# Moments and normalization of the first batch's x in the setup block, V's low weights on GpSimd, Wk loaded first

## What is computed

```
emb = silu(sin_emb(timestep)) @ W_ada + b_ada; scale, shift = split(emb)
x = ln(src) * (1 + scale) + shift
q, k, v = x @ Wq + bq, x @ Wk + bk, x @ Wv + bv
probs = softmax(where(mask, -inf, q k^T / sqrt(32) + attention_bias))
x = x + (probs v) @ Wo + bo
out = rotate(x + gelu2(ln(x) * g2 + beta2 @ W1 + b1) @ W2 + b2)
```

## Time and profile before

| | us |
|---|---|
| median of 3 runs | 3292.41 (3285.91 to 3293.02) |
| the profiled execution's own time | 3286.79 |
| its span | 3285.0 |
| PE busy | 3159.6 (96%) |
| POOL, DVE, ACT busy | 2015.2, 2141.5, 1859.9 |
| DMA queue of SP | 79.3% of the span |

### The profile page before, as it was taken

The page is one execution under the profiler, slowest core; times in us unless marked ns, Lnnn a source line. Parts: engine busy times, 40 slices in busy tenths (PEclk is TensorE's granted clock), DMA queues, the critical chain, the costliest instruction groups (busy, mean ns, idle before and its releaser), DMA issues. The chain is left out here.

```text
span 3285.0 us, 52375 instructions
## 1 busy us (share of the span) xinstructions
PE 3159.6 (96%) x16592; PEld 2373.3 (72%) x16592; DVE 2141.5 (65%) x4445; ACT 1859.9 (57%) x4041; POOL 2015.2 (61%) x1247
## 2 busy tenths in 40 slices
PE   5999999999999999999969999999999999999998
PEld 4777777777777777767638688787877868687787
DVE  3777778777777777877757654554645555464542
ACT  2777777777777777777725243342434434253443
POOL 3888888888878888878745633435333443434413
PEclk9999999999999999999989999999999999999999
DMA  5999999998999999998857677675767757586665
GB/s 188 263 267 272 261 274 279 263 265 270 261 271 267 268 261 264 275 270 261 259 157 269 211 246 222 188 254 180 256 205 221 243 185 247 181 261 207 200 204 166
DMA packets 440432, 785.15 MB, mean 239 GB/s; under 512 B 57024, under 2 KB 106176, under 8 KB 440160
## 3 DMA queue, kind: packets, MB, share of 16 engines
q1 hardware_dynamic: 440160, 781.82, 79.3%
HBM read 591.76 MB, written 89.19 MB: 207 GB/s over the span
## 5 line engine op out<-in xcount | busy, mean ns | idle before, releaser
L671 POOL TENSOR_TENSOR biasm<-biasm,maskb 128x1024 f32<-128x1024 f32 x512 | 1091.8, 2152 | 241.6 <-DMA biasm<-in_fside_Bx16xSxS_dram 238.4
L1388 PE MATMUL ps_out<-w_ring,g_hi 128*128 128x512 f32 x2048 | 678.7, 398 | 15.9 <-POOL w_ring L1625 7.9
L1368 PE MATMUL ps_first<-h_hi,w_ring 128*128 128x512 f32 x1792 | 553.4, 390 | 7.5 <-issue 7.4
L1607 POOL TENSOR_TENSOR g_lo<-g_now,g_hi 128x512 fp32r<-128x512 f32 x128 | 169.3, 1323 | 618.1 <-ACT g_hi L1485 618.1
L776 PE MATMUL ps_score<-k_rows,q_rows 96*128 96x512 f32 x1024 | 493.1, 482 | 3.7 <-issue 3.3
L1388 PEld LDWEIGHTS ps_out<-w_ring,g_hi 128*128 128x128 f32 x2048 | 385.6, 188 | 110.4 <-issue 30.8
L827 ACT ACTIVATE probT<-ps_probT 128x512 f32<-128x512 f32 x512 | 305.2, 596 | 239.6 <-PE ps_probT L789 162.2
L917 DVE CUSTOM_DVE_ANT_0 prob_first<-ps_score,biasm 128x512 f32<-128x512 f32 x512 | 346.9, 684 | 142.7 <-PE ps_score L776 104.0
L917 DVE CUSTOM_DVE_ANT_0 prob_last<-ps_score,biasm 128x512 f32<-128x512 f32 x512 | 346.5, 686 | 139.1 <-PE ps_score L776 109.6
L789 PE MATMUL ps_probT<-ident,prob_first 128*128 128x128 f32 x2048 | 392.9, 273 | 16.8 <-DVE probT L496 10.4
L1388 PE MATMUL ps_out<-w_ring,g_lo 128*128 128x512 f32 x1024 | 399.7, 390 | 0.0
(11 more groups left out here) (159 smaller groups left out, 5606.8 us busy)
## 6 DMA issues: line engine op xcount, KB each, us to landing
biasm<-in_fside_Bx16xSxS_dram SPq DMA_DIRECT2D x512, 512.0 KB, 7.2
w_ring<-w_parts SPq DMA_DIRECT2D x240, 512.0 KB, 3.7
w_ring<-w_parts SPq DMA_DIRECT2D x392, 256.0 KB, 3.5
k_rows<-k_hi SPq DMA_DIRECT2D x512, 64.0 KB, 6.0
q_rows<-q_hi SPq DMA_DIRECT2D x512, 64.0 KB, 4.0
xn<-in_x_dram SPq DMA_DIRECT2D x16, 1024.0 KB, 8.0
normal_rows<-xn SPq DMA_DIRECT2D x16, 1024.0 KB, 9.2
k_rows<-k_lo SPq DMA_DIRECT2D x256, 64.0 KB, 5.6
```

The costliest lines, as they stand in the source:

```text
L671: pool.tensor_tensor(tile, tile, maskb[:, 2 * half:2 * half + 2, :], ALU.add).then_inc(masked.sem, 1)
L1368: mm = pe.matmul(ps[:, BANK[n], :], w1r[:, place, w, cols], h[:, n, c, :], start=(c == 0 and k == 0 and not onto), stop=(c == 1 and k == 2 ...
L1388: mm = pe.matmul(ps_out[:, t, :], a[:, k % 2, cols], w2r[:, k % VR, w, :], start=(m == 0 and n == 0), stop=(m == NF - 1 and n == 2))
L1607: pool.tensor_tensor(GLO[:, k % 2, :], src, GHI[:, k % 2, :].bitcast(F32), ALU.subtract).then_inc(glo_done.sem, 1)
```

## The change

In the setup block, after the modulation's activations, DVE takes batch 0's moments, adds EPS, and, between K's low weights and Q's, normalizes `xn` in place; the power is POOL's. POOL also makes V's low weights. SP loads Wk ahead of Wq, and ACT and DVE treat K first (ACT scales Wq when its turn comes). START no longer does the moments, the power and the normalization of batch 0; the later batches are as before. DVE increments a semaphore where it has waited for the power (`dve_waited`, bookkeeping alone).

```diff
@@ setup_block, SP
                 load_x(sp, 0)
-                for n in range(3):
+                for n in (1, 0, 2):
                     sp.dma_start(wst[:, n, :, :], ...).then_inc(w_in[n], 16)
@@ setup_block, POOL
+                eps_added.wait(pool, -1, 0)
+                pool.tensor_tensor(rstd[:, :], var_eps[:, :], half_pow[:, :], ALU.pow).then_inc(pow_done.sem, 1)
+                pool.wait_ge(scaled, 1 + NC * 3)
+                for c in range(NC):
+                    pool.tensor_tensor(WL[2][:, c, :], wst[:, 2, c, :], WH[2][:, c, :].bitcast(F32), ALU.subtract)
@@ setup_block, DVE
-                for n in range(3):
-                    dve.wait_ge(scaled, 1 + NC * (n + 1))
+                x_in.wait(dve, -1, 0)
+                for t in range(NC):
+                    dve.bn_stats(stats[:, t, :], xn[:, t, :]).then_inc(stats_made.sem, 1)
+                stats_made.wait(dve, -1, NC - 1)
+                for t in range(NC):
+                    dve.bn_aggr(mean_var[:, t, :], stats[:, t, :]).then_inc(stats_done.sem, 1)
+                stats_done.wait(dve, -1, NC - 1)
+                dve.tensor_scalar(var_eps[:, :], mean_var[:, :, 1], EPS, None, ALU.add).then_inc(eps_added.sem, 1)
+                for n in (1, 0):
+                    dve.wait_ge(scaled, (1 + 2 * NC, NC)[n])
                     for c in range(NC):
                         dve.tensor_tensor(WL[n][:, c, :], wst[:, n, c, :], WH[n][:, c, :].bitcast(F32), ALU.subtract)
+                    if n == 1:
+                        pow_done.wait(dve, -1, 0)
+                        dve.sem_inc(dve_waited, 1)
+                        for t in range(NC):
+                            dve.tensor_scalar(xn[:, t, :], xn[:, t, :], mean_var[:, t, 0:1], rstd[:, t:t + 1],
+                                              ALU.subtract, ALU.mult).then_inc(normed.sem, 1)
@@ setup_block, ACT
-                act.wait_ge(w_in[0], 16)
-                act.mul(wst[:, 0, :, :], wst[:, 0, :, :], QSCALE).then_inc(scaled, 1)
-                act.wait_ge(scaled, 1)
-                for n in range(3):
+                for n in (1, 0, 2):
                     act.wait_ge(w_in[n], 16)
+                    if n == 0:
+                        act.mul(wst[:, 0, :, :], wst[:, 0, :, :], QSCALE).then_inc(scaled, 1)
+                        act.wait_ge(scaled, NC + 1)
                     for c in range(NC):
                         act.activation(WH[n][:, c, :], wst[:, n, c, :], ACT.Copy).then_inc(scaled, 1)
@@ attention_stage, POOL, START
-                    spread_of(-1)
-                    for t in range(NT):
-                        norm(-1, t)
                     for c in range(NC):
                         split_x(-1, c)
@@ attention_stage, DVE, START
-                    for t in range(NT):
-                        moments(-1, t)
-                    aggregate(-1)
```

More of the change, by code:

```diff
@@ L96, in setup_block @@
 def setup_block(nc, steps, theta, phi, W_ada, b_ada, W_qkv, b_qkv, freqs, ident, mod, rot, half_pow, WH, WL, bqk,
-                load_x):
+                load_x, x_in, xn, stats, mean_var, var_eps, rstd, stats_made, stats_done, eps_added, pow_done, normed,
+                dve_waited):
     B = steps.shape[0]
@@ L286, in load_mask @@
             .then_inc(mask_in.sem, 16)
+    stats = sb("stats", [P, NT, 6])
+    mean_var = sb("mean_var", [P, NT, 2])
+    var_eps = sb("var_eps", [P, NT])
+    rstd = sb("rstd", [P, NT])
+    pow_done = Tally(sem("pow_done"), 1)
+    eps_added = Tally(sem("eps_added"), 1)
+    stats_made = Tally(sem("stats_made"), NT)
+    stats_done = Tally(sem("stats_done"), NT)
+    normed = Tally(sem("normed"), NT)
     setup_block(nc, steps, theta, phi, W_ada, b_ada, W_qkv, b_qkv, freqs, ident, mod, rot, half_pow, WH, WL, bqk,
-                load_x)
+                load_x, x_in, xn, stats, mean_var, var_eps, rstd, stats_made, stats_done, eps_added, pow_done, normed,
+                dve_waited)
     xf = [sb("xf", [P, S]), mask_raw[:, :, :].rearrange("p t k -> p (t k)").bitcast(F32)]
@@ L312, in attention_stage @@
     rsumT = sb("rsumT", [P, S])
[L313 to L316, removed]
     bv_col = sb("bv_col", [P, NC])
@@ L347, in attention_stage @@
     mask_ready = Tally(sem("mask_ready"), 1)
[L348 to L352, removed]
     xt_done = Tally(sem("xt_done"), NC)
```

## The result

The kernel after takes **3260.92 us** (median of 6 runs, 3259.64 to 3266.41), the kernel before 3285.2 on the same chip (6 runs, 3279.08 to 3293.02). The ratio is 0.9927, with an interval of 0.9913 to 0.994: 24 us less, where the forecast had 3283.5 and a range that ended at 3276. The profiled run of after took 3259.64, with a span of 3257.2, so 27.8 us less span than before's 3285.0.

A forecast was written before the change was run, and what follows sets the result against it. PE was taken to bound the body. Setup's end +2.3, transposes' head start -10.9 and SP's store wait +2.5 gave -6.1 us: 3280.7 from the profile, 3286.3 from the median, forecast halfway at 3283.5, range 3276 to 3291.

The forecast's parts named there:

- The step that failed: Whole kernel: PE bounds the body, so a shorter start-up shifts all the rest by as much.
- The block's end, +2.3 us: Setup block: last work ends at 35.1 us, so the engines' meeting comes 2.3 us later (1.9 to 3.6).
- Transposes 8.6 us earlier: START: x's transposes begin at about 37.9 us against 46.55, and `k_lo` ends at 50.3.
- The store holds SP until 52.4: START: the store of normalized x lands at 52.4 us, so k(4)'s first rows go at 52.8, 2.5 after `k_lo`.
- The rival that it does not hold SP: START: the store lands by 50.3 us beside Wo, gain 8.6 us; chance 0.13.
- the thin tail of Wo: START: only 125 GB/s flowed in Wo's last us; the store may fill it and land up to 0.9 us earlier.
- Batch 1's x lands at 57.7, `q_lo` at 59.1, PE idle 5 us: START: x, behind the store, lands at 57.7 us, `q_lo` ends at 59.1, PE idles 5 us before k(5).
- The rival with x deciding: START: batch 1's x lands 3 us later than forecast, delaying `q_lo` and SP 2.4 us; gain 3.7; chance 0.2.
- The slow pace after a pause: k(5): after idling, matmuls come every 0.43 us for 3.2 us, then every 0.23, the clock column reading 1.00 at both.
- A start-up's lead is a gain: Start-up to total: the lead of 6.1 us (5.6 to 7.0) shortens the kernel by as much.
- GpSimd's subtractions over 1.7 us each: Setup block's end: a slower kernel, by 6.6 us if four subtractions take 4.5 us each; chance 0.03.
- The sign for a failed shift: Body, 150 to 1650 us: PE having more or fewer than 1470 us of work in 1500 would refute the shift.

The follow-up runs named there:

- e1: Kernel before with only the four small tensors declared ahead of `xf`, putting attention buffers on multiples of 256 bytes: 3263.64 us, ratio 0.9956 to before.
- e7: Changed kernel with SP's store of normalized x issued ahead of the bias loads: 3261.88 us, ratio 0.9941 to before.
- e6: Changed kernel again, unchanged, beside another set of runs of before: 3263.91 us, ratio 0.9943.
- e2: Changed kernel with 64 bytes more declared ahead of `xf`, so buffers lie 64 past a multiple of 256 again: 3277.9 us, ratio 0.9996 to before.
- e13: Transfers alone, 24 bias loads per offset: 403 GB/s at a multiple of 256, 385 to 388 at 32, 64, 128 and 192 past.
- e9: Kernel before with `negmax` and `bv_col` declared ahead of `xf`, so buffers lie 128 past a multiple of 256: ratio 0.9974 to before.
- e4: Kernel before with the four small tensors declared just ahead of `biasm`, so only `biasm` and `maskb` are aligned: ratio 0.9971 to before.
- e8: Changed kernel with `xn`, `mask_raw` and the feed-forward stage's buffers also on multiples of 256 bytes: ratio 0.9951 to before.
- e11: Changed kernel with GpSimd following V's high part copy by copy instead of waiting for all four: 3258.08 us, ratio 0.9928 to before.

## Why the prediction was wrong

**The step that failed** is the one that says "a start-up that is shorter by some us should shift all the rest by as much, and the question is only how far the start-up moves". The batches were taken as fixed since their programs are not edited. But the diff moves buffers, and a batch went from 99.2 to 97.9 us. The sum lacked a term: 15 batches by 1.3 us, 19.9 us in the profiles, and 14 to 15 us in the time of e1 (0.44%). The rest of the 28 us is the start-up's 5.6 and the 2.3 behind the last mask, which no run takes apart.

Point by point:
- *The block's end, +2.3 us*: right. 34.8 against 35.1, the loads at 36.09 against 36.4. DVE's last row for `bqk` took 1.23 us, more than the modulation's whole share in my sum, but lay beside GpSimd's subtractions.
- *Transposes 8.6 us earlier*: 8.9. `k_lo` ended at 48.85 instead of 50.3; PE left its slow pace sooner than I let it. The wait for the store covered that.
- *The store holds SP until 52.4*: right in place and cause, 52.31; e7 takes it away, and the rows come with `k_lo`. The rival that it does not hold SP is out. (The 0.9 us that the thin tail of Wo was to give back is nearer 0.7: in that us 263 of 388 GB/s were free, 388 being 1 MB in 2.7 us.)
- *Batch 1's x lands at 57.7, `q_lo` at 59.1, PE idle 5 us*: 57.97, 59.3 and 6.4 us. The rival with x deciding is what e6 came near: its first score is 2.8 us later.
- *The slow pace after a pause*: right in its cost, wrong in its reading of the clock. After 6.4 us without work in after, PE's matmuls came every 0.43 us from 59.96 to 62.95, and then every 0.23 (3.2 us of slow ones in the sum, 3.6 in the trace, from 59.37 on). The sum took its price from rows and stands. But the granted clock was not 1.00 at both paces: it was 0.50, the level of 1.2 GHz, while they were slow, and 1.00, the level of 2.4 GHz, from then on, in before as in after (0.50 from 60 to 62 us, 1.00 from 64 to 66), so the column and the pace do not contradict each other as the prediction had it. At one place the column does read 1.00 beside the slow pace, in before from 53 to 57 us; why was not found. Before, from 71 and from 74 us (the column behind the busy times is the granted clock):

```profile
71.00:73.00 2.00, 2.00 (x6) 1.58 (x5) 1.02 (x3) 0.81 (x2) 2.00 (x2) 0.50 0.46 113
74.00:76.00 2.00, 2.00 (x10) 1.63 (x9) 1.59 (x4) 0.70 (x2) 2.00 (x2) 1.00 0.42 102
```

- *A start-up's lead is a gain*: 5.6 us in the traces. In time it is smaller or unclear, so the forecast's 6.1 us is not borne out either: e6 against e1, nearly the same places, differ by 0.13% (4 us), each with as much to either side, and e2 against before by 0.04% (1 us, with an interval of 3 to either side).
- *GpSimd's subtractions over 1.7 us each*: they took 5.18 for four, 1.3 each. That rival is out.
- *What there was to gain*: the section on time puts some 50 us of PE's idle time into the first 80 us. By the trace PE is busy for 44.1 of these 80, so it is 36.
- *The sign for a failed shift* was the right question with a poor instrument: its window ran over the end of the stage. 150 to 1600, or the first and last mask conversion, show it at once.

**What stays open.** Why 128 past costs less than 64 in the kernel and all of the 4% in e13. In e9 one of the buffers, `rsumT`, came to stand on a multiple, and copies from SBUF to SBUF are in the kernel's queue, whose cost at each offset no run shows.

How 4% of a transfer become 1.3% of a batch is seen only in part. In the windows 150 to 1600 PE is idle for 25.5 us before and 14.8 after, which is 0.75 us of the 1.3 that a batch lost; the rest lies in the time that the profile counts as busy, and was not traced. The matmuls of both have the same lengths within 1.5%. The largest wait of PE there, in before and in after (us waited in total, times, longest):

```profile
PE ps_fill L730 <- POOL x_lo L640: 10.1, 10, 1.5
```

```profile
PE ps_fill L750 <- POOL x_lo L663: 5.5, 6, 1.6
```

It is tempting to read an order from this: a load lands late, GpSimd adds the mask late, what is queued behind it on GpSimd is late for PE. The other runs don't bear it out. In e6, with the kernel of after, PE waits 10.5 us for `x_lo` and the batches take 98.12 us; in e2, with the old places, it waits 2.8 us and they take 98.99. So that wait does not follow the places, and by which chain the transfers hold the batches up is open. That the place decides is shown (e1 to e4).

## What to carry to other kernels

Read the whole diff, declarations too, and compare the addresses of all buffers that a queue fills before you call a part of the program untouched; where the DMA queue is near full (0.95 here), try its buffers on multiples of 256 bytes of the partition; in the feed-forward stage, with a share of 68%, it gave nothing (e8). Test this first with a kernel that changes only the layout: it is one run, and it takes the accident out of every later comparison. For the length of a repeated piece take the first and the last of an instruction that each piece has once, not a window of fixed ends, which a faster kernel overruns.

## What the runs showed of the hardware

- In a long row of loads into SBUF, those that start off a multiple of 256 bytes of the partition ran at 385 to 388 GB/s instead of 403, the same at 32, 64, 128 and 192 past (e13); in the setup blocks the weights ran at 386 to 395 instead of 403 to 410 (eight and six runs). In this kernel the places were worth 0.44%, with no instruction changed (e1).
- DVE's and GpSimd's subtractions hold each other up: 5.72 us for DVE's four beside GpSimd's (e11), 2.50 where they overlap only at their end (after).
- In after a DVE instruction of 128 x 4 elements took 1.23 us beside GpSimd's subtractions, and 0.16 in before, with GpSimd idle.
- After a pause of 6.4 us (after) the granted clock was 0.50 and matmuls of 512 columns came every 0.43 us for 3 us; then it was 1.00 and they came every 0.23.
